# Gathers, masks and spread reciprocals of a paged-attention kernel moved between GpSimd, VectorE, ScalarE and the load queue

## What is computed

```python
x = x + einsum('bct,bcd->bdt', x, L0_weights[cond])        # a 32x32 mix of tokens per sequence, chosen of 200
x = x + attention(x, block tables, kv_lens)                # 8 query heads, 4 kv heads of 32, window of 128 keys
x = x + einsum('bsi,oi->bso', x, W_base) + lora(x)*scaling  # four adapters of rank 16, one per sequence
x = x + einsum('bct,bcd->bdt', x, L3_weights[subject])     # a 32x32 mix of tokens per sequence, chosen of 8
```

## Time and profile before

| | |
|---|---|
| three runs, us | 301.96, 302.19, 303.79 (median 302.19) |
| profiled execution, us | 302.65 |
| its span, first to last instruction | 300.8 |
| granted TensorE clock, mean | 0.905 of full |
| busy: PE, DVE, ACT, POOL | 70%, 69%, 44%, 55% |

### The profile page before, as it was taken

How to read it: one execution, slowest core, us unless ns; L and a number is a source line. 1 busy time by engine, 2 the same in 40 slices (tenths; PEclk the granted TensorE clock), 3 DMA queues, 4 the chain that set the end, 5 groups by cost and what they waited for, 6 DMA issues and landing times.

```text
span 300.8 us, 7985 instructions
## 1 busy us (share of the span) xinstructions
PE 210.8 (70%) x2402; PEld 155.9 (52%) x2402; DVE 209.0 (69%) x628; ACT 131.8 (44%) x491; POOL 164.2 (55%) x279
## 2 busy tenths in 40 slices
PE   0132599699899993005788876897868879988773
PEld 0112475455555551004667755675657667767641
DVE  0987947888699985204589876784884867878760
ACT  0220015155444553321756664465555744667510
POOL 4456856067555557754266666556656665673120
PEclk9999859799999998555799998997997998999998
DMA  5819995034611000023031434233424343331011
GB/s 151 258 34 209 211 381 112 17 107 136 194 55 46 29 20 35 32 64 97 4 111 55 118 89 129 73 110 93 142 58 113 95 128 74 115 104 58 20 37 35
DMA packets 18319, 29.70 MB, mean 99 GB/s; under 512 B 8189, under 2 KB 13640, under 8 KB 17906
## 3 DMA queue, kind: packets, MB, share of 16 engines
q0 software_dynamic: 7408, 19.04, 22.9%
q1 hardware_dynamic: 8130, 5.22, 6.0%
q10 hardware_dynamic: 2752, 5.08, 5.4%
HBM read 29.43 MB, written 7.34 MB: 122 GB/s over the span
## 4 chain that ended last, share of the span: by engine, by line
issue 28%; POOL 24%; PE 19%; DMA 16%; DVE 4%; POOLq 4%; ACT 3%; SPq 0%; ACTq 0%; DVEq 0%
DMA big<-in_pool,row_now 4%; DMA w0c<-in_w,w_i 4%; PE quad L1119 4%; POOL own L547 4%; PE quad L1171 4%; POOL big L482 3%; POOL work L504 3%; PE bank L1157 3%; POOL big L542 3%; DMA merged<-work,row_now 2%; POOLq L422 2%; POOL merged L517 2%; DMA big<-merged,row_now 2%; POOL w0c L436 2%; DMA con<-in_consts 2%
## 5 line engine op out<-in xcount | busy, mean ns | idle before, releaser
L699 ACT ACTIVATE work<-bank,nmx 128x164 f32<-128x164 f32 x128 | 49.6, 398 | 30.3 <-DVE nmx L981 24.7
L1157 PE MATMUL bank<-kt_rope,big 128*128 128x164 f32 x256 | 46.8, 319 | 0.0
L1157 PEld LDWEIGHTS bank<-kt_rope,big 128*128 128x128 f32 x256 | 43.4, 205 | 5.0 <-issue 0.8
L995 DVE TENSOR_TENSOR onT<-quad,rT 32x256 f32<-32x256 f32 x64 | 26.9, 420 | 21.9 <-PE quad L1171 20.4
L1153 PE MATMUL bank<-mask,identb 128*128 128x492 bf16 (+1 forms) x48 | 18.2, 379 | 30.3 <-DVE kt_rope L972 22.7
L981 DVE TENSOR_REDUCE nmx<-bank 128x3 f32<-128x492 f32 (+1 forms) x48 | 28.5, 593 | 12.3 <-PE bank L1157 12.1
L1119 PE MATMUL quad<-wqkv_sb,work 128*128 128x512 f32 x64 | 34.2, 660 | 2.8 <-ACT work L652 2.7
L988 DVE STREAM_TRANSPOSE work<-work 128x768 f32<-128x768 f32 (+2 forms) x96 | 34.7, 410 | 0.0
L682 ACT ACTIVATE big<-qT,con 128x256 f32<-128x256 f32 (+1 forms) x64 | 27.2, 512 | 0.1
L517 POOL DMA_INDIRECT merged<-work,row_now x16 | 18.3, 1141 | 15.4 <-ACT work L646 9.0
L436 POOL DMA_INDIRECT w0c<-in_w,w_i x16 | 16.9, 1054 | 17.9 <-DMA w0c<-in_w,w_i 7.1
(11 more groups left out here) (158 smaller groups left out, 469.6 us busy)
## 6 DMA issues: line engine op xcount, KB each, us to landing
merged<-big ACTq DMA_DIRECT2D x3, 1024.0 KB
xin<-in_x SPq DMA_DIRECT2D x16, 128.0 KB
out<-x4s SPq DMA_DIRECT2D x16, 128.0 KB, 2.0
w3bd<-in_w SPq DMA_DIRECT2D x64, 4.0 KB
con<-in_consts SPq DMA_DIRECT2D x1, 660.5 KB, 5.2
wqkv_sb<-in_wqkv ACTq DMA_DIRECT2D x1, 512.0 KB
wt_sb<-in_wt ACTq DMA_DIRECT2D x1, 256.0 KB
wp_sb<-in_wp ACTq DMA_DIRECT2D x1, 256.0 KB
```

The source lines that it names most:

```text
L699: act.activation(prob[:, p, hd, 0:NK], ps_sc[(p + i) % 2][:, j * NK:j * NK + NK], ACT.Exp, bias=nmx[:, p, hd:hd + 1], scale=1.0, accum_out ...
L995: ve.tensor_tensor(onT[rows, :, :].rearrange("p c (b n) -> p b c n", b=NB), ps_o[rows, :, 64 * (g % 2):64 * (g % 2) + 64].rearrange("p b ( ...
L1157: mm = pe.matmul(at[:, j * NK:j * NK + NK], qbd[:, p, hd, :], kT[:, p, hd // GSZ, 0:NK], start=False, stop=(j == n - 1), skip_group_check= ...
```

## The change

- `rwide` is written by ScalarE, in one instruction, between the result of the last layer and the exponents; GpSimd loses both copies.
- The masks of all 16 tiles are built by VectorE in two instructions at the end of phase 1, as zeros and ones in bf16; `identb` carries the factor -1e30. TensorE picks the tile's mask with a register.
- w3 + I is formed once, for all eight matrices, by VectorE while the indices are computed, written to a scratch in HBM and read from there by L394; GpSimd loses `w3i`. The buffer is free after the last layer's product, no longer after `w3i`.
- The gathers take their index columns straight from `idx`: GpSimd's steps of phase 2 are all written out, so the index copies L480 and L539 go.
- `cached` and `fetch` of one tile are one block behind the product with the values, four tiles ahead: old rows, `own`, a wait for the old rows, merged rows. `fetch` of the first four tiles goes ahead of the steps.

```diff
@@ sync
+            sp.dma_start(w3e[:, :, :], w3.rearrange("n c d -> c n d")).then_inc(s_w3e, 16)
...
+            sp.wait_ge(w3e_done, 1)
+            sp.dma_start(w3_d.rearrange("n c d -> c n d"), w3e[:, :, :]).then_inc(s_w3d, 16)
+            sp.wait_ge(s_w3d, 16)
...
-                        sp.wait_ge(w3i_done, t - 1)
-                    diagonal(t, p, w3, subj_sb, w3bd, s_w3)
+                        sp.wait_ge(l3_done, t - 1)
+                    diagonal(t, p, w3_d, subj_sb, w3bd, s_w3)
@@ gpsimd
             def cached(t, r):
-                pl.tensor_copy(row_now[:, 0, r:r + 1], idx[:, 0, bass.ds(t, 1)]).then_inc(row4_copied, 1)
-                wait(row4_copied, t + 1)
                 pl.indirect_dma_start(
                     out=kvb[:, r, :], out_offset=None, in_=pool_rows4,
-                    in_offset=bass.IndirectOffsetOnAxis(ap=row_now[:, 0, r:r + 1], axis=0),
+                    in_offset=bass.IndirectOffsetOnAxis(ap=idx[:, 0, t:t + 1], axis=0),
...
-                if isinstance(h, int) and NT <= 4 * h + u < NT + 2:
-                    masks(4 * h + u - NT, u % 2)
...
             def fetch(t, r, n):
+                pl.indirect_dma_start(
+                    out=own[:, r, :], out_offset=None, in_=merged_rows2,
+                    in_offset=bass.IndirectOffsetOnAxis(ap=idx[:, 2, t:t + 1], axis=0),
+                    bounds_check=SEGS * 8 - 1, oob_is_err=False, engine_sem=desc_fetch).then_inc(s_own[r], 16)
+                wait(desc_fetch, 2 * t + 1)
                 wait(s_cache[r], 16 * (n + 1))
                 pl.indirect_dma_start(
                     out=kvb[:, r, :], out_offset=None, in_=merged_rows4,
...
-            fetch(0, 0, 0)
-            fetch(1, 1, 0)
+            for t in range(RING):
+                fetch(t, t, 0)
+
+            for s in range(NT + 2):
+                t = s - 2
                 if valid(t):
                     wait(zs_done, t + 1)
+                    if t >= 1:
                         wait(l2_done, t)
                     pl.tensor_tensor(zm[0:E * R, :].rearrange("p (b c) -> p b c", b=NB),
...
+                t = s - 1
+                if valid(t) and valid(t + RING):
+                    wait(pv_done, t + 1)
+                    cached(t + RING, t % RING)
+                    fetch(t + RING, t % RING, t // RING + 1)
@@ scalar
-            act.copy(identb[:, :], ident).then_inc(s_prec, 1)
+            act.activation(identb[:, :], ident, ACT.Copy, scale=NEG).then_inc(s_prec, 1)
...
+                if valid(t1):
+                    act.wait_ge(rden_done, t1 + 1)
+                    if not isinstance(t1, int) or t1 >= 1:
+                        act.wait_ge(rT_done, t1)
+                    act.copy(rwide[:, :].rearrange("p (c g d) -> p c g d", c=GSZ, g=G),
+                             rden[:, 1 - p, :].rearrange("p (g c) -> p c g", c=GSZ).unsqueeze(3)
+                             .broadcast_to([128, GSZ, G, HD])).then_inc(rwide_done, 1)
@@ vector
+            ve.wait_ge(s_w3e, 16)
+            ve.tensor_tensor(w3e[:, :, :], w3e[:, :, :], cc("ident", TOK)[:, 0:TOK].unsqueeze(1)
+                             .broadcast_to([TOK, 8, TOK]), ALU.add).then_inc(w3e_done, 1)
...
+            for k, (name, a, b, op) in enumerate((("backpos", 0, NKB, ALU.is_lt), ("ownpos", NKB, NK, ALU.is_gt))):
+                ve.tensor_tensor(mask[:, :, a:b], cc(name).unsqueeze(1).broadcast_to([128, NT, b - a]),
+                                 pos3[:, k, :].unsqueeze(2).broadcast_to([128, NT, b - a]), op).then_inc(mask_done, 1)
             keys(0, 0, 0, 0)
@@ tensor
-                          mask[:, p, :].unsqueeze(1).broadcast_to([128, n, NK]), start=True, stop=False,
+                          mask[:, bass.ds(t, 1), :].broadcast_to([128, n, NK]), start=True, stop=False,
...
-                    pe.wait_ge(w3i_done, t3 + 1)
-                    pe.matmul(ps_l3, w3i[:, 1 - p, :], x3s[:, 1 - p, :], start=True, stop=True).then_inc(l3_done, 1)
+                    pe.wait_ge(s_w3[1 - p], 64 * (k3 + 1))
+                    pe.matmul(ps_l3, w3bd[:, 1 - p, :], x3s[:, 1 - p, :], start=True, stop=True).then_inc(l3_done, 1)
```

More of the change, by code:

```diff
@@ L168, in build @@
         w3bd = sb("w3bd", [128, 2, 128])
-        w3i = sb("w3i", [128, 2, 128])
+        w3e = sb("w3e", [TOK, 8, TOK])
         qsc = sb("qsc", [128, HD])
@@ L188, in build @@
         kT = kt_rope[:, 0:2 * G * KW].rearrange("p (a g k) -> p a g k", a=2, g=G)
-        mask = sb("mask", [128, 2, NK], BF16)
+        mask = sb("mask", [128, NT, NK], BF16)
         work = sb("work", [128, 7008])
@@ L346, in build @@
         on_used = sem("on_used")
-        s_blank, w3i_done = sem("s_blank"), sem("w3i_done")
+        s_blank = sem("s_blank")
+        s_w3e, w3e_done, s_w3d = sem("s_w3e"), sem("w3e_done"), sem("s_w3d")
         pT_done, pv_done, rden_done = sem("pT_done"), sem("pv_done"), sem("rden_done")
@@ L517, in phase1 @@
                     pl.indirect_dma_start(
-                        out=merged, out_offset=bass.IndirectOffsetOnAxis(ap=row_now[:, 3, r:r + 1], axis=0),
+                        out=merged, out_offset=bass.IndirectOffsetOnAxis(ap=row_now[:, r:r + 1], axis=0),
                         in_=kvrow[:, r, :], in_offset=None,
@@ L543, in fetch @@
                     out=kvb[:, r, :], out_offset=None, in_=merged_rows4,
-                    in_offset=bass.IndirectOffsetOnAxis(ap=row_now[:, 1, r:r + 1], axis=0),
+                    in_offset=bass.IndirectOffsetOnAxis(ap=idx[:, 1, t:t + 1], axis=0),
                     bounds_check=SEGS * 4 - 1, oob_is_err=False, engine_sem=desc_fetch).then_inc(s_merge[r], 16)
[L546 to L550, removed]
-                wait(desc_fetch, 2 * t + 2)
-            fetch(0, 0, 0)
-            fetch(1, 1, 0)
[L556 to L559, removed]
-                    if not isinstance(t, int) or t >= 1:
-                        wait(rT_done, t)
-                    for c in range(2):
-                        pl.tensor_copy(rwide[:, 128 * c:128 * c + 128].rearrange("p (g d) -> p g d", g=G),
-                                       rden[:, p, :].rearrange("p (g c) -> p c g", c=2)[:, c].unsqueeze(2)
-                                       .broadcast_to([128, G, HD])).then_inc(rwide_done, 1)
-                t, k, p, r, n = at_step4(h, u, 2)
+                wait(desc_fetch, 2 * t + 2)
+            for t in range(RING):
+                fetch(t, t, 0)
+            for s in range(NT + 2):
+                t = s - 2
                 if valid(t):
                     wait(zs_done, t + 1)
-                    if not isinstance(t, int) or t >= 1:
+                    if t >= 1:
                         wait(l2_done, t)
@@ L572, in phase2 @@
                                      zs[:, :].rearrange("p (b c) -> p b c", b=NB),
-                                     zscale[:, bass.ds(t * NB, NB)].unsqueeze(2).broadcast_to([E * R, NB, TOK]),
+                                     zscale[:, t * NB:t * NB + NB].unsqueeze(2).broadcast_to([E * R, NB, TOK]),
                                      ALU.mult).then_inc(zm_done, 1)
-                    wait(s_w3[p], 64 * (k + 1))
-                    if reused(t):
-                        wait(l3_done, t - 1)
-                    pl.tensor_tensor(w3i[:, p, :], w3bd[:, p, :], ident, ALU.add).then_inc(w3i_done, 1)
-                t, k, p, r, n = at_step4(h, u, -1)
-                if valid(t) and reused(t):
-                    wait(sc_done, 3 * (t - 1))
-                    masks(t, p)
-                t, k, p, r, n = at_step4(h, u, -2)
-                if valid(t):
-                    fetch(t, r, n)
-                t, k, p, r, n = at_step4(h, u, -3)
-                if valid(t) and (not isinstance(t, int) or t >= RING):
-                    wait(pv_done, t - 3)
-                    cached(t, r)
-            steps(pl, phase2, NT + 2, *P2R[1:])
+                t = s - 1
[3 more added lines that the diff above has]
+                    fetch(t + RING, t % RING, t // RING + 1)
         @block.scalar
@@ L1009, in phase2 @@
                     ve.wait_ge(exp_done, H * (t1 + 1))
+                    if reused(t1):
+                        ve.wait_ge(rwide_done, t1 - 1)
                     ve.reciprocal(rden[:, p1, :], den[:, p1, :]).then_inc(rden_done, 1)
@@ L1146, in scores @@
                     pe.wait_ge(qbd_done, NB * (t + 1))
-                    pe.wait_ge(mask_done, 2 * (t + 1))
+                    pe.wait_ge(mask_done, 2)
                 if i == 2:
```

20 lines of the change are left out of this document (5 added, 15 removed).

## The result

The changed kernel takes 282.24 us (median of 4 runs, 281.83 to 283.83) against 302.31 for the kernel before (4 runs): a ratio of 0.934 [0.929, 0.939]. The forecast was 281.0, with 276 to 288 as its range. The profiled execution is the longest of the four, 283.83 us with 3.1 of it outside its span; the other three lie 1.9 to 2.7 us above their spans. So I compare spans: 300.8 before, 280.7 after, 20.1 us less, against a forecast of 21.15.

A forecast was written before the change was run, and what follows sets the result against it. GpSimd was taken to bound phase 2 at 9.32 us a step. The terms +0.4 - 0.8 - 4.05 + 2.1 - 19.9 + 0.8 + 0.3 = -21.15 gave 281.5 from the profiled 302.65, so 281.0 for the median; range 276 to 288.

The forecast's parts named there:

- The loop of the other engines, 7.9 a step: Phase 2 without GpSimd's limit: a loop through VectorE, ScalarE and TensorE closing over two steps, 15.8 us.
- the 0.06 of a register: TensorE choosing masks by register in phase 2's looped steps: 0.8 us lost in all, bounds 0 to 4.6.
- the light step: Step from tile 13 to 14 before the change, GpSimd without gathers: 8.03 us, TensorE's full work, clock 1.00.
- The rule (7.9 + z)/2: Phase 2 step when GpSimd's gather block with `zm`, of length z, exceeds 7.9 us; z forecast 7.7 to 8.0.
- So GpSimd sets phase 2: Before the change GpSimd's work and waits, over nine us a step, set phase 2's 9.32 us step, not TensorE.
- Each landing counts now: GpSimd's new gather block fills 7.7 to 8.0 of the 7.9 us step, so every landing matters.
- Rival 1: Gather block takes GpSimd's old place: landings grow to 5.6, step 8.45, 6.6 us lost, 287.6 us; 17%.
- The spread on ScalarE: ScalarE writing `rwide` in phase 2 takes 0.43 us, fits a gap of 0.8 and costs nothing.
- The load queue: Phase 2's later w3 block loads delay the store behind them: 6.9 us against 8.1 available, covered by 1.2.
- The end, +0.3: Last short steps: the store of an earlier tile lands about when its buffer is wanted; 0.3 us lost, bounds 0 to 1.7.
- Ahead of the steps: Index stage 0.4 us lost, phase 1 index copies 0.8 gained, border 4.05 gained, masks holding GpSimd 2.1 lost.
- The mask instruction did hold GpSimd: At the phases' border VectorE's masks block GpSimd's last index copy (L513): 2.1 us lost, none if the copy comes first.

The follow-up runs named there:

- the masks alone: Kernel before with only VectorE's masks and TensorE's register for them: median 295.28 us, ratio 0.975.
- the three parts together: Kernel before with spread, masks and w3 + I moved, old gather order, loop and index copies kept: median 294.47 us, ratio 0.971.
- the spread alone: Kernel before with only the reciprocals' spread (`rwide`) moved to ScalarE: median 300.23 us, ratio 0.990.
- with the masks held back: Kernel after, with VectorE's masks waiting for GpSimd's last index copy of the scatters: median 281.12 us, ratio 0.926.
- the edited ones: Kernel after with one edit each: `zm` ahead of the old rows' wait, 0.930; masks after the last index copy, 0.926; store ahead of w3's blocks, 0.927.
- three kernels on one chip: Kernel after with masks by a constant, 287.27 us; one more ScalarE copy, 286.28 us; `zm`, mask-wait and store edits together, 285.12 us.

## Why the prediction was right, and where it was not

- **The total** holds: 20.1 us of span against 21.15, inside the forecast's own range. That it is off by only 1.05 is in part luck. The steps gave 2.85 less than forecast, and what lies ahead of X of tile 1 gave 1.13 more (3.48 against 2.35) and the end 0.67 more (0.37 less instead of 0.3 more).
- **The loop of the other engines, 7.9 a step**: right. Eleven of fourteen steps average 7.96, without the 0.06 of a register that no run shows, and TensorE waits for ScalarE's queries as in the light step of the earlier trace rows. The rule (7.9 + z)/2 for a late block gave 8.55 and 8.53 was measured.
- **"So GpSimd sets phase 2"**: right as to the engine; "on one engine that adds up to over nine" was only half of the reason. Beneath the work lies a chain through one landing, 9.5 us in the old order, that the sum hides. Removing the work alone gives steps of 9.29 (9.52 from tile 5 on), not 7.9. What shortens the chain, by the sum of its pieces, is that `own` is issued beneath the landing (1.8 us) and that the index copy goes (0.6), and only `zm` stands behind the block; the whole rearrangement is what the runs show. Since the prediction worked the new block out from its own chain (0.85 + 4.4 + 0.85 + 1.11 + 0.47), the number for the whole change was still right, but the expectations for the masks alone and for the three parts together, which went by the sum of work, were 9 and 12 us too low, and that for the spread alone 5. The sign was there: under full load 3.1 us of waiting for old rows were already left over the earlier trace rows.
- **Each landing counts now**: right in kind. One landing of 6.11 us cost 1.33 us; the size of the ordinary block, 7.3 to 8.2 us from X to the end of `zm` (7.7 forecast), just fits. The 4.73 us that the prediction took for the longest landing before is a piece of the chain; the landings of the earlier trace rows end at 4.4, which leaves the forecast as it was. Rival 1 (landings grown to 5.6 in every step) did not come: the median is 4.6.
- **The spread on ScalarE**: right, 0.40 us in the gap, nothing lost. Undoing it alone gives 9.86 a step.
- **The load queue, "covered by 1.2 us"**: mis-sized. One store landed after 4.3 us, where 3.7 was the longest before, and cost 0.49 us in the first profile; with the masks held back a step with one took 9.35, 1.4 over 7.96; in the kernel after run again (284.59 us) there were four such waits, and two steps with one took 9.05 and 9.44, together 2.6 us over twice 7.96. With the store ahead of the blocks none is left. The term stood at 0 in the steps; in the traces it is 0.5 to some 2.6, and the time does not tell it from nothing.
- **The end, +0.3**: from X of tile 15 to the end 10.5 us against 10.9, a small gain. But the step before it took 8.97 at the lower clock: 1.01 over 7.96, and 1.6 over the 7.37 that this step takes at clock 1.00 in other runs. No term held that. Why the clock fell in both profiles of the kernel after and in none of the edited ones was not tried.
- **So the steps**: forecast 14 x (9.32 - 7.96) = 19.1 us, measured 130.5 - 114.25 = 16.25. The difference, 2.85, is 0.49 (the store), 1.33 (the landing) and 1.01 (the clock in the last step).
- **Ahead of the steps**: forecast 0.4 - 0.8 - 4.05 + 2.1 = -2.35, measured at the keys of tile 1 -2.69. GpSimd's first instruction behind the indices came 0.06 us later, not 0.4: w3 + I found a gap. Its product at 112.93 before the border came 1.05 us earlier (forecast 0.4). From there to the keys 1.64 of the 1.95 forecast. One size was wrong there: the prediction kept the last landing before the keys at 3.5 us, as of `own` before, but now the merged rows come last, and they took 3.99. The mask instruction did hold GpSimd: 1.63 us of the copy, 2.1 forecast. The Trainium skill (SBUF — State Buffer, "Who interferes with whom") has the two exclude each other; the trace agrees, 1.81 against 0.18 us. It holds the copy here, and in the experiment in its place the scatter, which the prediction had left alone; there the measurement decides, 2.41 us. X of tile 0 gained 1.1 us more: its first product took 2.94 us at the border before, at clock 1.00 with a merged gather issued 1.14 us into it, and 1.64 after.

## What to carry to other kernels

When an engine is busy nearly the whole step, also follow the chain of its waits through one period with all its other work struck out; if that is as long as the sum, taking work away gives waiting. Of an order of DMAs ask for each landing what stands behind it in the same queue and could have been issued before it. And test a bundle by taking single parts away as well as adding them: here the part worth 1% alone carried the whole gain.

## What the hardware did that I had not expected

- An indirect scatter on GpSimd is held by a VectorE instruction of two SBUF operands too: 2.41 us instead of 0.98, in both kernels whose masks wait for the last index copy. The prediction had taken the scatter itself as free of this.
- The landing of 512 KB of old rows, 4.3 to 4.4 us before, has a median of 4.6 in the kernel after and reached 6.11 once (5.0 to 5.2 in four later profiles), and the stores' longest went from 3.7 to 4.2 to 4.4.
- The product with the values, 1.65 us at full clock, took 2.2 to 2.7, once 3.0, in twelve steps of three kernels on one chip, with a stop of about 0.25 us inside for which the trace names no releaser, and up to 2.1 in the kernel after. Each time an indirect gather was issued on GpSimd beside it. That this is the cause is likely and not shown.
